# Combine stage of a mixture-of-experts block: groups without products go inside another group's pass, their variance from VectorE's statistics; the last group by tiles

## What is computed

```
x = x + layernorm(attention(layernorm(x)))          # 8192 rows of 512
x = x + layernorm(ffn(layernorm(x)))                # what matters here
# ffn: per row 4 of 32 experts, y = sum w * (silu(x W1) * (x W3)) W2, plus the shared expert
#      silu(x sw1) * (x sw3) @ sw2, for every row
# layernorm(y) = (y - mean) / sqrt(var + 1e-5), over the 512 columns
```

## Time and profile before

| | us |
|---|---|
| median of 3 runs | 2073.93 (2068.39 to 2074.55) |
| profiled execution | 2071.74 |
| its span | 2069.9 |
| TensorE busy | 1821.6 (88%) |
| VectorE busy | 1180.3 (57%) |
| ACT busy | 1169.9 (57%) |
| POOL busy | 758.9 (37%) |

### The profile page before, as it was taken

How to read it: one execution, slowest core, us unless ns; L and a number is a source line. 1 busy time by engine, 2 the same in 40 slices (tenths; PEclk the granted TensorE clock), 3 DMA queues, 4 the chain that set the end, 5 groups by cost and what they waited for, 6 DMA issues and landing times.

```text
span 2069.9 us, 33813 instructions
## 1 busy us (share of the span) xinstructions
PE 1821.6 (88%) x12976; PEld 890.0 (43%) x12976; DVE 1180.3 (57%) x2199; ACT 1169.9 (57%) x1499; POOL 758.9 (37%) x718
## 2 busy tenths in 40 slices
PE   8999999999969998898788897547999998997775
PEld 5444444444438885133233333223444444443332
DVE  6776767676630000267888988863444443443775
ACT  5565655555436665587677876422444444442775
POOL 0000000000000000015677778875577777773110
PEclk9999999999979999999899999769999999999887
DMA  6435353537358886668768875454689999987994
GB/s 245 172 132 190 133 190 128 195 119 235 108 155 210 212 211 156 155 182 213 224 204 244 246 225 166 156 215 144 164 187 231 237 227 251 233 165 193 319 325 174
DMA packets 189905, 407.26 MB, mean 197 GB/s; under 512 B 33844, under 2 KB 72116, under 8 KB 173120
## 3 DMA queue, kind: packets, MB, share of 16 engines
q1 hardware_dynamic: 83184, 222.41, 36.0%
q10 hardware_dynamic: 69696, 126.36, 17.6%
q0 software_dynamic: 36864, 56.32, 14.5%
HBM read 237.06 MB, written 179.18 MB: 201 GB/s over the span
## 4 chain that ended last, share of the span: by engine, by line
PE 17%; DMA 13%; DVE 10%; issue 8%; ACT 6%; POOL 5%; SPq 1%; POOLq 0%; DVEq 0%; ACTq 0%
PE s_gates L1488 5%; PE s_ups L1488 4%; PE s_ys L1503 4%; DMA s_spread<-share_dram 4%; DMA acc_dram<-s_y,s_slot 3%; DMA den_dram<-s_den 2%; DMA s_rows<-rows_dram,s_slot 2%; POOL slot_dram L1260 2%; POOL acc_dram L1428 2%; ACT s_xT L1534 1%; ACT s_xT L1555 1%; PE s_turned L1465 1%; PE s_y L898 1%; DMA share_dram<-s_share 1%; ACT s_phi L967 1%
## 5 line engine op out<-in xcount | busy, mean ns | idle before, releaser
L258 PE MATMUL s_proj<-s_xT,keep_wqkv 128*128 128x512 f16 x1536 | 341.8, 379 | 0.0
L1260 POOL DMA_INDIRECT slot_dram<-keep_filled,keep_slots x256 | 292.3, 1142 | 101.1 <-issue 70.8
L1428 POOL DMA_INDIRECT acc_dram<-s_y,s_slot x128 | 204.5, 1597 | 94.1 <-issue 35.2
L258 PEld LDWEIGHTS s_proj<-s_xT,keep_wqkv 128*128 128x128 f16 x1536 | 147.8, 98 | 183.1 <-issue 12.6
L898 PE MATMUL s_y<-keep_wo,s_at_hl 128*128 128x512 f16 x768 | 189.8, 400 | 34.4 <-ACT s_z L988 34.4
L1626 DVE SCALAR_TENSOR_TENSOR s_h<-s_gate,s_ups 128x512 f32<-128x512 f32 x96 | 65.9, 687 | 223.7 <-ACT s_gate L1543 220.8
L339 POOL TENSOR_SCALAR s_rstd<-s_mv 128x4 f32<-128x4 f32 x16 | 16.0, 999 | 458.8 <-DVE s_mv L354 458.8
L676 ACT ACTIVATE s_phi<-s_logits 128x1024 f32<-128x1024 f32 x128 | 131.1, 1024 | 83.8 <-PE s_logits L697 83.8
L1543 ACT ACTIVATE s_gate<-s_gates 128x512 f32<-128x512 f32 x96 | 56.9, 593 | 209.4 <-PE s_ups L1488 209.3
L237 PE MATMUL s_proj<-keep_wqkv,s_xT 128*128 128x512 f16 x768 | 173.9, 384 | 1.2 <-ACT s_xT L500 1.2
L518 ACT ACTIVATE s_hl<-s_rot 128x1024 f16<-128x1024 f32 x64 | 67.6, 1057 | 178.7 <-DVE s_rot L400 170.0
(11 more groups left out here) (174 smaller groups left out, 3233.5 us busy)
## 6 DMA issues: line engine op xcount, KB each, us to landing
s_x<-x_in SPq DMA_DIRECT2D x32, 1024.0 KB, 12.4
qk_dram<-s_hl ACTq DMA_DIRECT2D x32, 1024.0 KB, 6.5
keep_ahead<-qk_dram SPq DMA_DIRECT2D x48, 512.0 KB
acc_dram<-s_zero SPq DMA_DIRECT2D x17, 1024.0 KB, 15.6
v_dram<-s_v ACTq DMA_DIRECT2D x16, 1056.0 KB, 7.3
s_v<-v_dram SPq DMA_DIRECT2D x16, 1056.0 KB, 11.0
s_spread<-share_dram SPq DMA_DIRECT2D x64, 256.0 KB
x_dram<-s_x ACTq DMA_DIRECT2D x16, 1024.0 KB
```

Of the source, the lines that this page charges most:

```text
L258: mm = nc.tensor.matmul(out[:, 512 * b:512 * b + 512], left, right, start=(c == 0 and i == 0), stop=(c == EC - 1 and i == 2))
L1260: nc.gpsimd.indirect_dma_start(out=io["slot"], out_offset=bass.IndirectOffsetOnAxis(ap=slots[n % 2][:, a * K + j:a * K + j + 1], axis=0), ...
L1428: nc.gpsimd.indirect_dma_start(out=io["acc"], out_offset=bass.IndirectOffsetOnAxis(ap=slot[e % RING][:, a, 0:1], axis=0), in_=y[e % 2][:, ...
```

## The change

There are 12 units now, one for each group with a product. Four units have two places: a group without products comes first in the pair and is handled within the unit of the other. The order of the groups is changed so that groups 0 to 3 stand at places 1, 4, 7 and 10.

- For places 1, 4, 7, 10 and 15 (`BY_STATS`) VectorE measures: `measure`, a bn_stats for each tile, and `aggregate`, four bn_aggr, give mean and variance. `sum_up`, the tile of zeros, and for these five `center` and `square` are gone.
- VectorE in a unit: hidden 0, low 0, measure and aggregate of the early group, shift of the last group of the unit before, include 0 and 1, hidden 1, include 2 and 3, center, low 1, shift of the early group, add for each group of the unit before (one or two).
- ACT in a unit: square of the last group of the unit before, silu and high 0, the stores of the unit two before, scale of two tiles, silu and high 1, scale of two tiles, then four scales of the early group.
- The last group (place 15): each include is followed by its measure; then aggregate, add(14), its shift; scale, add (`add_tile`) and store (`store_last`, 256 KB each) go tile by tile.
- `sums`, `rstd` and `shift` have four buffers instead of two; `z_ready` counts tiles.

The diff, cut to its core (in SP's program nothing is edited, but it follows `ORDER`):

```diff
-        ORDER = (4, 5, 0, 6, 7, 1, 8, 9, 2, 10, 11, 3, 12, 13, 14, 15)
+        ORDER = (4, 0, 5, 6, 1, 7, 8, 2, 9, 10, 3, 11, 12, 13, 14, 15)
+        UNITS = ((0,), (1, 2), (3,), (4, 5), (6,), (7, 8), (9,), (10, 11), (12,), (13,), (14,), (15,))
+        BY_STATS = (1, 4, 7, 10, 15)
...
+        RANK = 4
+        ROUND = [len([r for r in range(q) if (r in BY_STATS) == (q in BY_STATS)]) for q in range(NG)]
+        centre, var = t.pair("centre", [P, A]), t.pair("var", [P, A])
+        sums, rstd, shift = ([t.sb(f"{n}{k}", [P, A]) for k in range(RANK)] for n in ("sums", "rstd", "shift"))
+        power, stats, mv = t.sb("power", [P, A]), t.sb("stats", [P, A, 6]), t.pair("mv", [P, A, 2])
         squares = xT[0][:].rearrange("p s c q -> p (s c q)").bitcast(F32).rearrange("p (a e) -> p a e", a=A)
...
             def make_rstd(q):
-                k = q % 2
-                pool.wait_ge(squared, q + 1)
-                if q >= 2:
-                    pool.wait_ge(z_ready, q - 1)
-                nc.gpsimd.tensor_scalar(rstd[k][:], var[k][:], 1e-5, None, ALU.add).then_inc(var_ready, 1)
+                k, i = q % RANK, ROUND[q]
+                if q in BY_STATS:
+                    pool.wait_ge(mv_ready, i + 1)
+                    variance = mv[i % 2][:, :, 1]
+                else:
+                    pool.wait_ge(squared, i + 1)
+                    variance = var[i % 2][:]
+                if q >= RANK:
+                    pool.wait_ge(z_ready, A * (q - RANK + 1))
+                nc.gpsimd.tensor_scalar(rstd[k][:], variance, 1e-5, None, ALU.add).then_inc(var_ready, 1)
                 pool.wait_ge(var_ready, q + 1)
                 nc.gpsimd.tensor_tensor(rstd[k][:], rstd[k][:], power[:], ALU.pow).then_inc(rstd_ready, 1)
...
-            def scale(q):
+            def scale(q, tiles):
                 act.wait_ge(shift_ready, q + 1)
-                at, k = total[q % ACCS], q % 2
-                for a in range(A):
-                    ins = nc.scalar.activation(at[:, a, :], at[:, a, :], ACT.Identity, bias=shift[k][:, a:a + 1],
-                                               scale=rstd[k][:, a:a + 1])
-                ins.then_inc(z_ready, 1)
+                at, k = total[q % ACCS], q % RANK
+                for a in tiles:
+                    nc.scalar.activation(at[:, a, :], at[:, a, :], ACT.Identity, bias=shift[k][:, a:a + 1],
+                                         scale=rstd[k][:, a:a + 1]).then_inc(z_ready, 1)
...
+            def store_last():
+                n, r = ORDER[NG - 1], (NG - 1) % X1S
+                for a in range(A):
+                    act.wait_ge(out_ready, NG + a)
+                    act.dma_start(io["out"][n * G + a * P:n * G + (a + 1) * P, :], x1[r][:, a, :]).then_inc(out_stored[r], 16)
...
-            for q, n in enumerate(ORDER):
-                p = NE + n
-                more = n >= NS and p + 1 < PASSES
-                if q >= 1:
-                    square(q - 1)
+            done = []
+            ready = []
+            for u, unit in enumerate(UNITS):
+                p = NE + ORDER[unit[-1]]
+                more = p + 1 < PASSES
+                if ready:
+                    square(ready[-1])
                 if more:
                     silu(p + 1, 0)
                     make_high(p + 1, 0)
-                if q >= 2:
-                    store(q - 2)
-                if q >= 1:
-                    scale(q - 1)
+                for q in done:
+                    store(q)
+                if ready:
+                    scale(ready[-1], (0, 1))
                 if more:
                     silu(p + 1, 1)
                     make_high(p + 1, 1)
-            square(NG - 1)
-            store(NG - 2)
-            scale(NG - 1)
-            store(NG - 1)
+                if ready:
+                    scale(ready[-1], (2, 3))
+                for q in unit[:-1]:
+                    scale(q, range(A))
+                done, ready = ready, unit
+            for q in done:
+                store(q)
+            for a in range(A):
+                scale(NG - 1, (a,))
+            store_last()
...
-            def sum_up(q, a):
-                at = total[q % ACCS][:, a, :]
-                dve.wait_ge(acc_loaded[q % ACCS], 16 * (q // ACCS) + 16)
-                nc.vector.scalar_tensor_tensor(out=at, in0=at, scalar=1.0, in1=nothing, op0=ALU.mult, op1=ALU.add,
-                                               accum_out=sums[q % 2][:, a:a + 1]).then_inc(summed, 1)
+                                               op1=ALU.add, accum_out=sums[q % RANK][:, a:a + 1]).then_inc(y_copied, 1)
+
+            def measure(q, a):
+                if ORDER[q] >= NS:
+                    dve.wait_ge(y_copied, A * (NE + ORDER[q]) + a + 1)
+                else:
+                    dve.wait_ge(acc_loaded[q % ACCS], 16 * (q // ACCS) + 16)
+                if a == 0 and ROUND[q] >= 1:
+                    dve.wait_ge(mv_ready, ROUND[q])
+                nc.vector.bn_stats(stats[:, a, :], total[q % ACCS][:, a, :]).then_inc(stats_ready, 1)
+
+            def aggregate(q):
+                dve.wait_ge(stats_ready, A * (ROUND[q] + 1))
+                for a in range(A):
+                    ins = nc.vector.bn_aggr(mv[ROUND[q] % 2][:, a, :], stats[:, a, :])
+                ins.then_inc(mv_ready, 1)
 
             def center(q):
-                n, k = ORDER[q], q % 2
-                if n >= NS:
-                    dve.wait_ge(y_copied, A * (NE + n) + A)
+                dve.wait_ge(y_copied, A * (NE + ORDER[q]) + A)
+                nc.vector.tensor_scalar(centre[ROUND[q] % 2][:], sums[q % RANK][:], -E ** -1.5, None,
+                                        ALU.mult).then_inc(centre_ready, 1)
+
+            def make_shift(q):
+                k = q % RANK
+                dve.wait_ge(rstd_ready, q + 1)
+                if q >= RANK:
+                    dve.wait_ge(z_ready, A * (q - RANK + 1))
+                if q in BY_STATS:
+                    mean, part = mv[ROUND[q] % 2][:, :, 0], -1.0
                 else:
-                    dve.wait_ge(summed, A * (len([m for m in ORDER[:q] if m < NS]) + 1))
-                nc.vector.tensor_scalar(centre[k][:], sums[k][:], -E ** -1.5, None, ALU.mult).then_inc(centre_ready, 1)
-
-            def make_shift(q):
-                k = q % 2
-                dve.wait_ge(rstd_ready, q + 1)
-                if q >= 2:
-                    dve.wait_ge(z_ready, q - 1)
-                nc.vector.scalar_tensor_tensor(out=shift[k][:], in0=sums[k][:], scalar=-1.0 / E, in1=rstd[k][:], op0=ALU.mult,
+                    mean, part = sums[k][:], -1.0 / E
+                nc.vector.scalar_tensor_tensor(out=shift[k][:], in0=mean, scalar=part, in1=rstd[k][:], op0=ALU.mult,
                                                op1=ALU.mult).then_inc(shift_ready, 1)
...
+            def add_tile(q, a):
+                r = q % X1S
+                dve.wait_ge(z_ready, A * q + a + 1)
+                dve.wait_ge(x1_loaded[r], 16 * (q // X1S) + 16)
+                nc.vector.tensor_tensor(x1[r][:, a, :], x1[r][:, a, :], total[q % ACCS][:, a, :],
+                                        ALU.add).then_inc(out_ready, 1)
...
-            dve.wait_ge(up_ready, IC * (NS + NE))
-            nc.vector.memset(nothing, 0.0).then_inc(nothing_set, 1)
-            dve.wait_ge(nothing_set, 1)
-            for q, n in enumerate(ORDER):
-                p = NE + n
-                more = n >= NS and p + 1 < PASSES
+            ready = []
+            for unit in UNITS:
+                q = unit[-1]
+                p = NE + ORDER[q]
+                more = p + 1 < PASSES
                 if more:
                     hidden(p + 1, 0)
-                if q >= 1:
-                    make_shift(q - 1)
+                    low(p + 1, 0)
+                for early in unit[:-1]:
+                    for a in range(A):
+                        measure(early, a)
+                    aggregate(early)
+                if ready:
+                    make_shift(ready[-1])
+                include(q, 0)
+                if not more:
+                    measure(q, 0)
+                include(q, 1)
                 if more:
-                    low(p + 1, 0)
-                if n >= NS:
-                    include(q, 0)
-                    include(q, 1)
-                    if more:
-                        hidden(p + 1, 1)
-                    include(q, 2)
-                    include(q, 3)
+                    hidden(p + 1, 1)
                 else:
-                    for a in range(A):
-                        sum_up(q, a)
-                center(q)
+                    measure(q, 1)
+                include(q, 2)
+                if not more:
+                    measure(q, 2)
+                include(q, 3)
                 if more:
+                    center(q)
                     low(p + 1, 1)
-                if q >= 1:
-                    add(q - 1)
+                else:
```

(10 more changed lines are left out.)

17 lines of the change are left out of this document (7 added, 10 removed).

## The result

| | before | after |
|---|---|---|
| median, us (9 runs each, side by side) | 2073.48 | 2059.82 |
| ratio, 95% interval | | 0.9946 (0.9928 to 0.9965) |
| profiled execution, us (span) | 2071.74 (2069.9) | 2064.81 (2063.0) |
| first include of the combine, us | 1900.63 | 1902.37 |
| from there to the end of the span ("the stage"), us | 169.27 | 160.63 |

The kernel became faster by 0.5%, and the predicted 2065 lies 5 us above the median. I compare stages and not whole spans in what follows. The first include waits for a load whose time the code ahead of the stage decides. Over kernels with the same code ahead of it, it started anywhere between 1892.9 and 1914.1 us. That scatter has nothing to do with the change, and it lies in every median.

The account below looks back on a forecast made before the run. The prediction took the alternating order of VectorE's and ACT's queues, which makes TensorE wait, as the bound. 2071.74 - 6.7 (middle) - 3.7 (tail) + 2.8 (clock) = 2064.1, stated as 2065 us, range 2055 to 2075.

Parts of the forecast that it names:

- an alternation of queues with some falls of the clock: Last stage: VectorE's and ACT's in-order queues wait for each other alternately, three clock falls cost 2.8 us; chance 0.66.
- pair to single: From include 0 of a pair's unit to that of the single unit behind it: 13.4 us, through ACT's scales and squares.
- single to pair: From a single unit's include 0 to the next pair's: 14.1 us, through two VectorE adds and the measuring.
- unit 13, unit 14: Last two units: include 0 at +11.3 after two adds, then at +10.3 after ACT's squares and silu.
- one wait of 6 becomes two of 3: TensorE in the middle: waits of 2.9 and 3.6 us replace 6.02; three groups take 27.5 instead of 29.08 us.
- at most every second unit: Clock falls in units 2 to 8: at most four, 3.8 us, since a slow stretch shortens the next wait to 1.4.
- the step that reads the length of a wait as deciding: TensorE's clock: no fall after 1.74 us idle, a fall after 2.72, so waits of 2.9 and 3.6 may cause one.
- POOL is done by +7.9: Tail: POOL finishes by 7.9 us after group 14's shift, so the last shift waits only for VectorE's add, until +8.5.
- The cover for the loads: Loads of sums are sent some three groups, over 20 us, ahead of use, so measures waiting for loads cost nothing.
- (1): Last stage: queues overlap fully and TensorE sets the pace, 10.54 us per unit, giving 2036 us; chance 0.08.
- (2): Middle: the clock falls in each of the seven units, costing 6.6 us, giving 2068, with the median 2070; chance 0.18.
- (3): Middle: the clock stays low through the whole next pass, TensorE becomes the bound, +25 us, giving 2090; chance 0.08.

Follow-up runs that it names:

- after again: The changed kernel unedited, seven runs on another chip: median 2067.98 us against 2076.92 for the kernel before, ratio 0.996; stage 158.18 us.
- e2: The changed kernel with bn_stats of places 1, 4, 7, 10 over 8 of 512 columns (no valid layernorm, only times count): 2050.85 us, stage 150.92.
- e5: The changed kernel with ACT's four scales of the early group moved one by one into gaps of the next unit: 2065.07 us, stage 149.2.
- e1: The changed kernel with its last group whole again (squares, one add, one store), group 14's store ahead of the squares on ACT: 2070.18 us, tail 24.6.
- e6: e1 with ACT's last squares put ahead of the store of group 14, as in the kernel before: 2066.33 us, stage 160.57, tail 20.6.
- e8: The changed kernel with group 14's add behind the last shift and its store behind the last scales: 2059.16 us beside 2077.19 before, tail 19.5.
- e3: The changed kernel with eight unused matmuls ahead of the third down tile in places 3 to 12: 2052.39 us, stage 157.69.
- v1: The changed kernel with early scales on ACT and the four measures on VectorE both spread into gaps: median 2052.78 us against 2076.92 before, ratio 0.9877.
- v2: v1 with SP's residual loads one place later, behind the next load of sums: median 2045.13 us against 2076.22 before, ratio 0.9862, stage 142.71.
- e4: The changed kernel with pairs kept but their early groups handled by row sums, centre and ACT squares, without statistics: 2082.86 us, stage 179.56.
- v3: v2 with the add of group 14 cut into four adds of 512 elements: median 2049.8 us against 2077.19 before, ratio 0.9859, tail 18.3 us.

## Why the prediction was right

The forecast was "an alternation of queues with some falls of the clock", and that is what the trace shows, by its own steps. After again stands for the same queues without a fall:

| step | forecast | measured |
|---|---|---|
| first include to that of unit (1, 2) | 13.7 | 13.68; 14.31 in after again |
| pair to single | 13.4 | 13.29 once, 14.0 to 14.4 three times with a fall; 13.29 each time in after again |
| single to pair | 14.1 | 14.01 twice, 14.29 with a fall; 14.01 each time in after again |
| unit 13, unit 14 | 11.3, 10.3 | 11.24, 10.53 |
| first include to shift of group 14, no fall of the clock | 140.5 | 140.25 (after again) |
| falls of the clock | 3, 2.8 us | 4, 3.0 us; none in after again; 0 to 1.0 us in the other runs with this middle |
| last shift but one to the end | 18.4 | 18.0 |
| sum, profiled execution | 2064.1 | 2064.81 |

That the sum is met within 0.7 us is in part luck. The first include came 1.74 us later than before, for no reason in the change; the middle was 0.6 and the tail 0.4 shorter than forecast. And the execution profiled lost more to the clock than any other with this middle.

**The two chains.** Where no fall comes in between, both intervals came within 0.1 us, from starts of successive instructions and the order of two queues, without any estimate of overlap. e2 and e5 show that they are different chains, since each shortens one interval by far more than the other: taking 2.09 us of measuring off VectorE shortens single to pair by 2.11; taking four scales from between include and square on ACT shortens pair to single from 13.29 to 10.53 (twice; the other two are TensorE's). The small rest of 0.1 is the pitch between includes, 0.61 and not 0.69 (1929.34 to 1929.95 in the trace). The price of measuring, 2.81 by the earlier trace rows, was 2.80, so its bounds of 2.4 and 3.1 weren't needed. The 10.3 for unit 14 was a slip: it is below the 10.54 of TensorE's own pass, which the prediction had counted, and 10.53 came.

**Which part of the change earns.** The prediction gave the 6.7 us of the middle to the new order as a whole. It didn't ask what the statistics would bring in the old rounds, and there the runs say more than it did: statistics alone 27.6 us for three groups, with pairs 27.3 without and 28.3 with the falls, pairs alone 32.6, before 29.3. The sum is right, but its reading as "one wait of 6 becomes two of 3" is not where most of the gain lies. Most of it is ACT's four squares for each early group off the path. Why the pairs bring so little is in the two traces above: each of their units is bound by the other queue, the pair's include waits behind two adds and all four measures, the single's behind four scales and four squares.

**The clock.** Four intervals of the first execution are longer than 13.29 or 14.01, by 0.28 + 0.92 + 0.72 + 1.09 = 3.0 us, where the forecast had 0.94 for one fall and three of them. The mechanism is the forecast's: the cost is what the slow matmuls leave at the next include, and the low stretch shortens the next wait. Three things were off. The second of the four came right behind the first, after a wait of only 2.07 us, so "at most every second unit" wasn't strict. And the step that reads the length of a wait as deciding failed: about the same 3.47 us were followed by eight matmuls in 3.59 in one execution and in 1.90 in the other. What decides it wasn't found.

The third is the price of a fall. The forecast put every fall at eight matmuls in 3.33 us and 0.94 on the chain, but a fall can cover only a part of the eight. TensorE after the same wait, in e1 and in e6, whose middle has the same queues:

```profile
2000.01 3.00 PE L1512 MATMUL s_ys<-s_sw,s_parts 128*128 128x512 bf16 x8 [3.47 <-DVE s_y L1680]
```

```profile
2000.63 2.40 PE L1512 MATMUL s_ys<-s_sw,s_parts 128*128 128x512 bf16 x8 [3.47 <-DVE s_y L1680]
```

The interval behind it is 13.79 us in e1 and 13.29 in e6. In the repeating part of after and e1 the interval grows by what the eight take beyond 2.5 us (3.59 us: 1.09; 3.41: 0.92; 3.23: 0.72; 3.00: 0.50; 2.76: 0.26; 2.64: 0.13). In e6 and e8 the granted clock is 0.94 from 1930 to 2014, the eight never take more than 2.44, and no interval grows there; only the last fall of e8 runs on into the matmuls of the short unit 13 and makes that one 1.0 us longer. So over the six executions with this middle, e3 with its fillers among them, the falls cost 3.0, 0.9, 1.0 and three times 0 us. The forecast's 2.8 is at the upper end of that. It fits the execution that was profiled first, by luck, and not the usual one.

**The tail.** Forecast 3.7, measured 4.1 us; the working had errors that cancelled: the last store left 0.6 us later than forecast, and landed in 2.1 us where the forecast had 2.9 to 4.3. The step "POOL is done by +7.9" failed: GpSimd was kept out by the add of group 14, and the last shift came at +9.4, not +8.5. In the kernel before no rstd had met an add, so no row of it showed this. The Trainium skill has it, page "SBUF — State Buffer", section "SBUF: two separate sides": VectorE and GpSimd share one pair of ports, and a VectorE instruction with two inputs from SBUF locks it for its whole length against a GpSimd instruction that reads SBUF. The trace agrees (2.17 us beside the large add, 0.58 beside a small one, 0.23 alone). I had not weighed it; by it the last shift would have stood about a microsecond later, an estimate from the add's end at +8.5 and GpSimd's second instruction of 1.04 us. The error cost the forecast nothing, if the end hangs on the issue of store 14 as I read it, which came at +8.2, and the forecast had +8.6. And of the 4.1 us, 1.5 are the low clock of the last tiles before (e6), which the measures now hide; the edit by itself is worth 2.6.

**Edits at nothing.** The cover for the loads held, with one include waiting for a load, the first. v1 shows how thin it is: at three groups in 24.5 us a load queued behind another's wait costs 2.8 us. The four small adds cost nothing, as the forecast said: 2.81 us for the four, at the pace of the scales. Against the page "VectorE: DVE Perf Modes" of the Trainium skill, section "The TRN2 errata — SBUF-src ops pay a fixed extra latency per instruction", e8 shows the price: back to back the four take 2.49 us and one of 2048 takes 2.29, so 0.2 us and not the 0.47 that its formula gives.

**The rivals.** (1), full overlap with 10.5 us for each unit, was not what this order does, but another order gets about two thirds of the way there: v2's units are 10.5 to 12.6 us in the repeating part. (2), a fall in each unit, didn't come: four of seven units in one execution, none in the other. (3), a clock that stays low and makes TensorE the bound, didn't happen in the kernel after; a small form of it is in e4 (1.00 us at one include) and e5 (12.1 and 12.2 us instead of 10.5).

**The median.** The stage gained 8.6 and 11.1 us in the two profiled executions, the medians differ by 13.7 and 8.9. The executions behind the medians have no trace, so where the difference lies isn't shown. The first include, which scatters over 21 us between profiled executions, is the likely place, and I have no cause for it.

## What to carry to other kernels

Where two in-order queues wait for each other in turn, busy shares say nothing of the pace: write both queues down, instruction by instruction with start-to-start times, and find for each interval the one chain that closes it; then move work out of that chain, between instructions that wait anyway. Bundling two units shortens little if the bundle puts its work in one lump ahead of what the other engine needs; the same work spread in the gaps, with the loads one place ahead (v2), took 16 to 18 us more out of the middle. And when the pace rises, look at what stands in the load queue behind somebody else's wait, before the loads become what is late.

## What the runs showed of the hardware

- The clock's fall isn't decided by the length of the last wait. Waits of 3.47 us were followed by eight matmuls in 3.59 us (after), 3.00 (e1) and 2.40 (e6), one of 3.48 by eight in 1.90 (after again); 3.23 us by eight in 1.90 (e6), 2.72 by eight in 3.33. Beside eight idle matmuls in each unit, with waits of 1.03 and 1.74 us left, the granted clock stayed at 1.00 for no cost (e3); that they kept it there isn't shown.
- bn_stats has little fixed cost: four of 512 columns take 2.46 us, four of 8 columns 0.37 (e2).
- GpSimd's small instruction took 0.23 us alone (e8), up to 2.17 beside a VectorE add of 2048 elements, until that add ended, and 0.58 beside adds of 512 (v3).
- A 256 KB store landed in 2.1 us, a 1 MB store in 4.3 us; a quarter issued right behind the megabyte took 4.2 (e8).
